# A graph network in one kernel: the late adjacency scatters, now waited for one by one with four in flight

## The reference

```
x = layernorm(x + L0(x, src, dst))             # softmax over the edges of a node
x = layernorm(x + L1(x, src, dst, edge_attr))  # message MLP, sum over the edges of a node
x = layernorm(x + L2(x, src, dst))             # two mean-aggregating convolutions, relu between
x = layernorm(x + L3(x, src, dst))             # two mean-aggregating convolutions, elu between

def conv(h):                                    # L2 and L3, twice each
    agg = segment_sum(h[src], dst) / max(degree, 1)
    return agg @ Wl.T + b + h @ Wr.T
```

## Time and profile before

| what | us |
|---|---|
| median of three runs | 4440.56 |
| profiled execution, first to last instruction (the span) | 5171.8 |
| late scatters in it, first to last start | 3268.4 to 3787.8 |
| POOL busy in it | 2510.8 (49%) |
| PE busy in it | 3159.9 (61%) |
| DVE busy in it | 2679.3 (52%) |

### The profile page before, as it was taken

How to read it: one execution, slowest core, us unless ns; L and a number is a source line. 1 busy time by engine, 2 the same in 40 slices (tenths; PEclk the granted TensorE clock), 3 DMA queues, 4 the chain that set the end, 5 groups by cost and what they waited for, 6 DMA issues and landing times.

```text
span 5171.8 us, 61853 instructions
## 1 busy us (share of the span) xinstructions
PE 3159.9 (61%) x18737; PEld 2317.1 (45%) x18737; DVE 2679.3 (52%) x5868; ACT 1560.3 (30%) x3684; POOL 2510.8 (49%) x2587
## 2 busy tenths in 40 slices
PE   1555555554755555555555554111159999999999
PEld 0333333333534344344344333100047777788777
DVE  4888888888645555555555556300001254433333
ACT  1777777776222222222222222100000011111000
POOL 7666666664666666666666666777720000000000
PEclk9999999999986667667667666555579999999999
DMA  5555555555134444444444443100037666666776
GB/s 183 192 198 191 195 194 194 192 192 164 56 98 111 112 121 111 116 117 111 114 118 112 111 118 85 58 0 0 13 126 282 215 218 245 247 248 251 259 276 228
DMA packets 387596, 797.88 MB, mean 154 GB/s; under 512 B 207412, under 2 KB 264600, under 8 KB 361128
## 3 DMA queue, kind: packets, MB, share of 16 engines
q1 hardware_dynamic: 239330, 586.35, 33.9%
q0 software_dynamic: 82320, 90.28, 7.9%
q10 hardware_dynamic: 65718, 118.62, 6.2%
HBM read 581.03 MB, written 213.92 MB: 154 GB/s over the span
## 4 chain that ended last, share of the span: by engine, by line
PE 25%; issue 23%; SPq 19%; DVE 3%; another core or an unknown queue 1%; DMA 0%; ACTq 0%; ACT 0%; DVEq 0%; POOL 0%
PE ps L1181 18%; SPq L626 14%; PE ps L1111 6%; SPq L601 1%; SPq L596 1%; SPq L622 1%; SPq L607 1%; SPq L617 1%; PE ps L1064 1%; ACTq L64 0%; DMA area<-adj 0%; PE ps L1083 0%; PE ps L1056 0%; DVE second L1650 0%
## 5 line engine op out<-in xcount | busy, mean ns | idle before, releaser
L770 POOL DMA_INDIRECT area<-src_table,early x784 | 752.5, 960 | 469.6 <-remote 225.5
L770 POOL DMA_INDIRECT area<-relu_table,early x784 | 739.6, 943 | 421.3 <-issue 212.4
L953 PE MATMUL ps<-ident,area 96*128 96x96 f32 x2352 | 441.4, 356 | 804.3 <-issue 555.4
L953 PEld LDWEIGHTS ps<-ident,area 96*128 96x128 f32 x2352 | 355.2, 213 | 939.2 <-issue 782.4
L1181 PE MATMUL ps<-second,area 128*128 128x288 bf16 x5194 | 652.1, 286 | 0.2 <-DVE second L1823 0.2
L1682 DVE TENSOR_TENSOR_SCAN area<-flags,area,ps 96x512 f32<-96x512 int8 x196 | 250.0, 1276 | 647.6 <-issue 552.0
L1181 PEld LDWEIGHTS ps<-second,area 128*128 128x128 f16 x5194 | 509.0, 98 | 128.5 <-DVE second L1823 0.5
L1650 DVE SCALAR_TENSOR_TENSOR second<-second,area,ps 128x512 bf16<-128x512 f32 x784 | 538.1, 741 | 0.0
L857 POOL DMA_INDIRECT adj<-out_ring x390 | 395.5, 1014 | 127.8 <-issue 127.8
L781 POOL DMA_INDIRECT adj<-copies_ring,cell_ring x392 | 388.6, 991 | 125.6 <-issue 118.9
L1111 PE MATMUL ps<-early,area 128*128 128x288 bf16 x2401 | 322.0, 292 | 204.9 <-issue 204.9
(11 more groups left out here) (330 smaller groups left out, 4709.0 us busy)
## 6 DMA issues: line engine op xcount, KB each, us to landing
area<-adj SPq DMA_DIRECT2D x147, 1632.0 KB
area<-adj SPq DMA_DIRECT2D x55, 1568.0 KB
adj<-early SPq DMA_DIRECT2D x102, 816.0 KB
soft_sums<-out_ring ACTq DMA_DIRECT2D x196, 384.0 KB
second<-key_dram SPq DMA_DIRECT2D x98, 512.0 KB
area<-dst_table SPq DMA_DIRECT2D x784, 48.0 KB
sums<-out_ring ACTq DMA_DIRECT2D x196, 192.0 KB
second<-caps_dram SPq DMA_DIRECT2D x98, 192.0 KB
```

Source lines behind the costliest of these rows:

```text
L770: pool.indirect_dma_start(out=src_rows[:, s, c, :], out_offset=None, in_=gather_table[p], in_offset=bass.IndirectOffsetOnAxis(ap=src_cols[ ...
L953: last = nc.tensor.transpose(ps[:, b, c * F:(c + 1) * F], r[:, (s * CH + c) * P:(s * CH + c + 1) * P], ident[0:F, 0:F])
```

## The change

POOL no longer waits batch by batch. The number of semaphores goes from two to four (`DEPTH`), scatter c uses semaphore c modulo 4, and ahead of each scatter c from the fifth on POOL waits until scatter c - 4 has landed. `adj_ready` still gets one unit for each eight landed scatters, now as soon as POOL has seen the eighth land, which is ahead of the fourth scatter after it. After the last scatter POOL waits for the last four.

```
-        late_made, adj_ready = [sem(f"late_made{b}") for b in range(2)], sem("adj_ready")
+        late_made, adj_ready = [sem(f"late_made{b}") for b in range(DEPTH)], sem("adj_ready")
...
-                    def batch_done(i):
-                        begun = sum(min(BATCH, SCATTERS - EARLY - k * BATCH) for k in range(i % 2, i + 1, 2))
-                        pool.wait_ge(late_made[i % 2], 16 * begun)
-                        pool.sem_inc(adj_ready, 1)
+                    def scattered(c):
+                        pool.wait_ge(late_made[c % DEPTH], 16 * (c // DEPTH + 1))
...
-                    for i in range(BATCHES):
-                        for c in range(i * BATCH, min((i + 1) * BATCH, SCATTERS - EARLY)):
-                            pool.indirect_dma_start(
-                                out=adj_all, out_offset=bass.IndirectOffsetOnAxis(ap=cell_late[:, c:c + 1], axis=0),
-                                in_=copies_late[:, c:c + 1], in_offset=None).then_inc(late_made[i % 2], 16)
-                        if i:
-                            batch_done(i - 1)
-                    batch_done(BATCHES - 1)
+                    for c in range(SCATTERS - EARLY):
+                        if c >= DEPTH:
+                            scattered(c - DEPTH)
+                            if (c - DEPTH + 1) % BATCH == 0:
+                                pool.sem_inc(adj_ready, 1)
+                        pool.indirect_dma_start(
+                            out=adj_all, out_offset=bass.IndirectOffsetOnAxis(ap=cell_late[:, c:c + 1], axis=0),
+                            in_=copies_late[:, c:c + 1], in_offset=None).then_inc(late_made[c % DEPTH], 16)
+                    for c in range(SCATTERS - EARLY - DEPTH, SCATTERS - EARLY):
+                        scattered(c)
+                        if (c + 1) % BATCH == 0 or c + 1 == SCATTERS - EARLY:
+                            pool.sem_inc(adj_ready, 1)
```

More of the change, by code:

```diff
@@ L37 @@
 BATCH = 8
+DEPTH = 4
 MATRICES = ["W0", "W_node", "W_src", "W_dst", "W_ef"]
```

## The result

The changed kernel takes 4511.99 us (median of 4 runs, 4503.87 to 4512.84) against 4440.56 before: a ratio of 1.0157, 95% interval 1.0145 to 1.0169. It is 71 us slower. The direction and the cause are the forecast's; the size lies 22 us above its middle, inside its own range of 4449 to 4525.

The account below looks back on a forecast made before the run. POOL's late scatters, 1.27 us each, were taken to bound the stage, with PE waiting for fills. 4440.56 + 49 us of stands (44 x 1.0 + 5) = 4490 us; this case alone 4449 to 4525, overall range 4425 to 4560.

Parts of the forecast that it names:

- The 731 us: Whole kernel: profiled execution 5171.8 us against median 4440.56, the excess put down to recording load (284 PE lateness, 424 "remote" waits).
- The wait per batch costs nothing, two more semaphores neither: POOL's late scatters: removing the batch wait gains nothing, since scatter 16's gap is the usual 0.30 us; added semaphores cost nothing.
- Alone, a scatter lands in 2.03 us, so the cap does not bind: Late scatters without a fill: landing 2.03 us after issue, under the 4.11 us available, with 2.08 us to spare.
- Beside a fill it lands 5.9 us after its issue, and POOL stands 1.8 us for it: Scatter whose issue ends as a fill begins: 2.03 + 3.9 us of hold, against 4.11 us available.
- On average 1.3 us, taken as 1.0, times 44: POOL's stands at 44 later fills: averaged over where a fill begins; with 5 us for the first four fills, 49 us.
- the first burst: First four fills, going out together within the first twelve to fifteen scatters: three rounds of four at 1.8 us, 5 us.
- Turns between the queues: DMA engines alternating queues packet by packet: a scatter beside a fill would wait about 1 us and land in 3 us.
- The units of `adj_ready` come earlier, worth nothing: Batch reports to SP come 6 us earlier except the last two; no gain at the end while POOL sets the pace.
- Nothing to see: Rival: packets take turns so the cap never binds, or late PE hides the stands; about 4437 to 4448 us, chance 0.25.
- Relief: Rival: fewer scatters in flight free a PE slowed by them; faster, 4156 to 4430 us, chance 0.15.
- the 2.80 us per product: PE's pace beside late scatters in the first profile, against 0.12 us each afterwards; forecast took it for an effect of recording.
- Much slower: Rival: every late scatter lands after 10.2 us, so POOL stands 6.4 us per four, 620 us; up to 5060, chance 0.07.

## Why the prediction was right, and where not

- **The 731 us.** The cause given is not borne out. They were put down to recording; other recorded executions took 4430.1 us before and 4511.1 after. But the stretched one lacks four fifths of its landings' records, so what its recording did is open. The sketch of the timed execution was right all the same: a stage of POOL's at 1.27 us a scatter (forecast 390 x 1.27 = 495, measured 505.9), PE ready and waiting for fills (in the changed kernel from tile 17 on, forecast about 24), and some 25 us from the last scatter to the end of the first convolution (30 us, from 3340.2 to 3370.6 in the kernel before, the late landing of the last scatter among them).
- **The wait per batch costs nothing, two more semaphores neither.** Right: eight in flight with eight semaphores is at 0.9989 and 0.9992 of before. That both lie a little below 1 is at the limit of what was measured. The kernel before has three gaps in its undisturbed stage that those of eight in flight lack, of 3.29, 1.69 and 1.70 us at scatters 113, 225 and 337 (from 0), none of them ended by a landing; whether they are the difference is open.
- **Alone, a scatter lands in 2.03 us, so the cap does not bind.** Right in what follows, too long as a size: the median is 1.1 us, and by the run with two in flight it is not over 1.57 (column 389 apart).
- **Beside a fill it lands 5.9 us after its issue, and POOL stands 1.8 us for it.** Right: 5.9 us in the chain's piece at 3230.64, and 2.05 us of stand behind it. That the sum fits so well is luck in part. Its terms were 2.03 alone and 3.9 of hold; measured, they are 1.1 and, by what is left, 4.8.
- **On average 1.3 us, taken as 1.0, times 44.** This is the term that was mis-sized. It measured (73.8 - 4.4) / 44 = 1.58 us, where 4.4 are the stands of the first burst (1.34 and 3.06; forecast 5). The average supposed that a fill may begin anywhere in a scatter's period. That holds for the first 13 of the 44 alone. Waits of SP and POOL in the changed kernel, from 2890 to 2976 and then from 2976 to 3417:

```profile
SPq L666 <- PE ps L1114: 98.2, 14, 36.8
POOL adj L859 <- DMA adj<-out_ring: 20.1, 14, 2.6
...
SPq L669 <- POOLq L858: 398.2, 31, 21.4
POOL adj L859 <- DMA adj<-out_ring: 63.0, 32, 2.7
```

  In the first stretch SP waits for PE to free a slot, and a fill begins anywhere: 20.1 - 14 x 0.30 = 15.9 us of stands, 1.2 us a fill, near the 1.3. In the second SP waits for POOL's report of a unit. POOL reports as a scatter lands, so the fill begins at the same place of the scatters' beat nearly each time: 53.4 us of stands for 31 fills, 1.7 us each. Twenty-four us ahead of the fill in the rows above, another goes out at 3206.48, and the next issue again starts 0.19 us later. The stands stand eight scatters apart, at 3213.61, 3225.56 and 3237.78, with 2.17, 2.08 and 2.35 us idle. The scatter that is hit there is one that is held for nearly the whole fill. The prediction had the upper end right: 44 x 1.8 + 5 = 84 us; 1.6 in place of 1.0 gives 75 us, against 71 measured.
- **Turns between the queues.** The Trainium skill, DMA: Bandwidth & Descriptors, section on queues, rings and completion order, has the engine go from queue to queue, a whole packet at a time. The prediction took the profile's packets for these and so had a scatter wait for one or two of a fill's. The trace shows no turns of that size: 70 packets of the fill and none of POOL's in 3 us. But a packet of the Trainium skill, in the same section, is typically 9 to 17 descriptors. A fill is 144 of the profile's packets, nine for each of 16 engines; if an engine's nine make one packet in that sense, the rule gives the hold that was seen. No run here tells which reading holds.
- **The units of `adj_ready` come earlier, worth nothing.** Not tested by itself. Six and eight in flight report a unit two scatters apart, 2.5 us, and take the same time to 0.2 us, which fits.
- **The rivals.** "Nothing to see" falls by the ratio, by stands at the first burst (1.64 and 3.36 us of idle time), and since PE is not late. "Relief" falls with the 2.80 us per product, which the undisturbed kernel before doesn't have either. "Much slower" falls by the median landing of 2.1 us from the issue's start without fills.

## What to carry to other kernels

The room that a cap on transfers in flight leaves is to be compared with the longest landing in the stretch where it binds, here some 6 us beside a 1.6 MB fill, not with the 1.1 us of a quiet queue: with six in flight (6.65 us of room) the cap is free, with five (5.38) it costs 0.3 us at every fill. Where the disturbing transfer is released by the very engine that it disturbs, it can meet the same instruction each time: ask for the price in that phase (here 1.7 us a fill), not for the mean over phases (1.2). And where a profiled execution is much longer than the timed ones, take another profile of it before any of its waits is explained.

## What the runs showed of the hardware that was not expected

- An execution can be stretched with no change to the kernel: 5171.8 us for a kernel of 4440, with one product of PE per 2.80 us beside the late scatters, and a fifth of the usual records of landings in its trace.
- A small scatter issued as a fill starts is held until the fill is nearly through: no packet of POOL's queue between 3232 and 3235, and landing 5.9 us after the issue in place of 1.1.
- POOL passes waits and reports while earlier scatters have yet to be issued: the issue at 3230.64 is number 265 of the late ones, the unit's report stands in the program ahead of number 267 and is seen at 3230.3, and the fill that it releases is out at 3230.44.
- One scatter of 390 is landed 10 us later than the others (11.67 us from its issue's start), and moves with its column, not with its place; with it at the front, the scatter issued behind it is late too.
